# Four small attentions of a perceiver network: exponentials by head on ScalarE, groups of four heads, division on the output, and one barrier fewer per stage

## The reference

```python
def layer_norm(x):
    ...
    return (x - mu) / jnp.sqrt(var + EPS)
def pattention(x, K, V):                 # K, V: 256 rows, for f 1024 rows
    a = softmax(EMB ** -0.5 * einsum('btc,nc->btn', x, K)); return einsum('btn,nc->btc', a, V)
def causal_sdpa(q, k, v):
    scores = einsum('bhqd,bhkd->bhqk', q, k) / sqrt(d)
    scores = where(tril, scores, -inf); attn = softmax(scores); return einsum('bhqk,bhkd->bhqd', attn, v)
h = layer_norm(x_in)                     # k, q, v = pattention(h, kK, kV), (h, qK, qV), (h, vK, vV)
...                                      # o = causal_sdpa(q, k, v); x2 = x_in + pattention(o, pK, pV)
...                                      # y = x2 + pattention(layer_norm(x2), fK, fV)
```

```python
scores = jnp.einsum('bhqd,bkd->bhqk', q, k) / sqrt(128)
scores = jnp.where(causal, scores, finfo.min)
attn = jnp.einsum('bhqk,bkd->bhqd', softmax(scores), v)
return attn.transpose(...).reshape(...) @ Wo
```

## Time and profile before

| | us |
|---|---|
| three runs | 1778.31, 1773.97, 1777.92 |
| median | 1777.92 |
| profiled execution | 1778.89, span 1777.1, mean TensorE clock 0.881 |
| PE / DVE / ACT / POOL busy | 1433.1 (81%) / 1001.7 (56%) / 700.0 (39%) / 96.5 (5%) |

### The profile page before, as it was taken

One profiled execution on the slowest core, in us unless ns is written; L12 is line 12 of the kernel. 1 busy time (PEld: TensorE's weight loads), 2 busy tenths in 40 slices (PEclk: granted clock), 3 DMA queues, 4 the chain that ended last, 5 costly groups with the idle time before them and its releaser, 6 DMA issues. The chain is left out here.

```text
span 1777.1 us, 28179 instructions
## 1 busy us (share of the span) xinstructions
PE 1433.1 (81%) x10760; PEld 1067.2 (60%) x10760; DVE 1001.7 (56%) x2900; ACT 700.0 (39%) x1524; POOL 96.5 (5%) x90
## 2 busy tenths in 40 slices
PE   7999999776598447799999999999983654647975
PEld 6979889554376233367776777777762532445763
DVE  5645444584565312277777777777756945343333
ACT  5735445212121110167667667666761010112211
POOL 2300000000000210200000000001000000000000
PEclk9999999888799659799999999999996565658997
DMA  9944333100331749410000000000002007007810
GB/s 320 327 164 160 118 111 140 53 1 20 139 131 56 249 153 350 180 59 33 33 33 33 33 33 33 33 32 33 2 1 116 1 0 301 0 0 261 277 57 4
DMA packets 61783, 181.15 MB, mean 102 GB/s; under 512 B 7249, under 2 KB 41169, under 8 KB 60369
## 3 DMA queue, kind: packets, MB, share of 16 engines
q1 hardware_dynamic: 56864, 156.77, 24.7%
q0 software_dynamic: 4352, 16.78, 2.6%
q10 hardware_dynamic: 432, 5.80, 0.8%
HBM read 178.68 MB, written 0.66 MB: 101 GB/s over the span
## 5 line engine op out<-in xcount | busy, mean ns | idle before, releaser
L1733 ACT ACTIVATE cross_s<-cross_s,cross_shift 128x896 f32<-128x896 f32 x224 | 215.1, 1031 | 35.2 <-DVE cross_shift L1813 35.2
L1727 ACT COPY cross_eT<-cross_ring 128x512 f32<-128x512 f32 x280 | 153.2, 591 | 144.9 <-PE cross_ring L1653 144.9
L1653 PE MATMUL cross_ring<-consts,cross_s 128*128 128x128 f32 x1568 | 199.4, 280 | 8.7 <-ACT cross_s L1733 8.7
L1653 PEld LDWEIGHTS cross_ring<-consts,cross_s 128*128 128x128 f32 x1568 | 170.7, 142 | 59.1 <-issue 43.8
L1804 DVE CUSTOM_DVE_ANT_0 cross_s<-cross_scores,cross_mask,cross_top 128x448 f32<-128x448 f32 x224 | 141.3, 680 | 84.3 <-PE cross_scores L1645 84.3
L374 ACT ACTIVATE slots_probs<-slots_scores,slots_bias,ctx_rinv 128x128 f32<-128x128 f32 x294 | 130.2, 460 | 109.0 <-DVE slots_bias L418 109.0
L1804 DVE CUSTOM_DVE_ANT_0 cross_s<-cross_scores,cross_mask,cross_half_max 128x448 f32<-128x448 f32 x224 | 141.3, 681 | 18.8 <-PE cross_scores L1645 18.8
L134 PE MATMUL slots_scores<-slots_qkT,slots_ctxT 128*128 128x128 f32 x1176 | 139.8, 277 | 9.1 <-DMA slots_ctxT<-in_ctxT 8.2
L134 PEld LDWEIGHTS slots_scores<-slots_qkT,slots_ctxT 128*128 128x128 f32 x1176 | 138.3, 194 | 13.0 <-DMA slots_ctxT<-in_ctxT 9.2
L324 PE MATMUL slots_attended<-ctx_rows,slots_probs 128*128 128x257 f32 x588 | 135.2, 380 | 1.4 <-DVE slots_pooled L432 1.4
L1645 PE MATMUL cross_scores<-cross_keysT,cross_qz 32*128 32x448 f32 x896 | 119.0, 589 | 0.8 <-DVE cross_keysT L1778 0.8
(11 more groups left out here) (742 smaller groups left out, 2114.3 us busy)
## 6 DMA issues: line engine op xcount, KB each, us to landing
slots_ctxT<-in_ctxT SPq DMA_DIRECT2D x42, 896.0 KB, 4.6
ctx_rows<-in_ctx_rows SPq DMA_DIRECT2D x28, 896.0 KB, 7.6
padded_ctxT<-in_ctxT SPq DMA_DIRECT2D x14, 896.0 KB, 4.6
cross_ctxT<-in_ctxT SPq DMA_DIRECT2D x14, 896.0 KB, 4.6
plain_ctxT<-in_ctxT SPq DMA_DIRECT2D x14, 896.0 KB, 4.7
ring_w<-in_moe_w POOLq DMA_DIRECT2D x12, 1024.0 KB, 17.8
ring_w<-in_moe_w SPq DMA_DIRECT2D x12, 1024.0 KB, 11.8
local_layers<-in_w_local SPq DMA_DIRECT2D x2, 4806.0 KB, 15.3
```

The lines of the kernel that those rows point to most:

```text
L1653: last = pe.transpose(bank(("turn", u, t))[:, j * P:(j + 1) * P], s_buf[:, u % 2, j, t * P:(t + 1) * P], K.ident)
L1727: act.copy(eT[:, u % 2, t], bank(item)).then_inc(st("emptied_act"), 1)
L1733: act.activation(rows, rows, ACT.Exp, bias=shift[:, u % 2, j:j + 1], scale=SCALE).then_inc(st("exp"), 1)
```

## The change

1. The second barrier at a stage's end is gone. GpSimd alone clears the semaphores after the block's barrier, and a new stage takes none of the numbers that the stage before it used (`semaphore()`, `Stage.cleared`).
2. `root_table` issues one square root, whose result nobody reads, at the end of ScalarE's stream in eleven stages; after it the set with Sqrt is the one loaded. The program has 45 table loads before and after.
3. In the four attentions the maximum (negated) is taken per group of four heads (`maxima_vector`), ScalarE reads the scores from PSUM and writes each head's exponential with that head's maximum as bias (`exponentials_scalar`: 16 in patt and in folded; 8 per layer in local and 8 in mqa, these with the sum in `accum_out`), TensorE turns a group as soon as its four are there (`turn_group`), VectorE copies it (`copies_vector`), and TensorE multiplies the group before it (`attend16`). Scores are scaled in a copy that was there anyway (hT, qT, oT, kT). The causal mask is added by TensorE: a product of identity and mask into the bank with `stop=False`, then the scores with `start=False`. The division moves to o: in patt and folded v has a 17th column of ones, whose product is the sum (`outputs16`); in local o is multiplied by the reciprocal of the sums. In mqa the probabilities are still divided, per group.
4. Patt: the two layer norms are one (one ScalarE call takes both square roots), the k, q, v, p and f softmaxes use bias and `accum_out`, f by halves; the quantising is cut into six pieces, 42 steps, dealt out by `Q_SPLIT`. The counts of idle products change: 4 at the start (5 before), none in front of the transposes of k, q, v and probabilities, later 2, 4, 3 for 3, 3, 9 and 1.
5. Folded: GpSimd fetches three slots of the ring; the fourth is fetched by SP at the start of moe. v is copied by ScalarE. Idle products are added: 4 at the start, 14 before the transposes of q and k, 3 after, 18 while o is away.
6. Local: masks and 16 idle products before the rotated q and k are turned, 3 after the scores; the copy of qkT in two parts. Mqa: masks and 2 idle products at the start, 4 after the scores, the last products by halves.

The core of the diff (patt's, folded's and local's streams to the part that is used below):

```diff
@@ Stage
     def __exit__(self, kind, *_):
         if kind is None:
-            self.nc.clear_and_free_semaphores(list(self.sems.values()))
-            self.nc.all_engine_barrier()
+            mine = list(self.sems.values())
+            Stage.cleared = [s.num for s in mine]
+            self.nc.clear_and_free_semaphores(mine)
         self.mem.close()
...
+def root_table(act, K):
+
+    act.activation(K.unused, K.ident[:, 0:1], ACT.Sqrt)
...
+def exponentials_scalar(act, st, tag, e, src, top, of, groups):
+
+    per = of // groups
+    for g in range(groups):
+        act.wait_ge(st(f"{tag}_top"), g + 1)
+        for h in range(g * per, (g + 1) * per):
+            last = act.activation(e[:, h], src[:, h], ACT.Exp, bias=top[:, h:h + 1])
+        last.then_inc(st(f"{tag}_exp"), 1)
+
+
+def maxima_vector(dve, st, tag, src, top, groups):
+
+    per = top.shape[1] // groups
+    for g in range(groups):
+        some = slice(g * per, (g + 1) * per)
+        dve.wait_ge(st(f"{tag}_scores"), g + 1)
+        dve.tensor_reduce(top[:, some], src[:, some], X_AXIS, ALU.max, negate=True).then_inc(st(f"{tag}_top"), 1)
...
+def attend16(pe, K, st, tag, heads, headsT, pr, prT, v, o_mm):
+
+    def attend(g):
+        pe.wait_ge(st(f"{tag}_probsT"), g + 1)
+        for hd in range(4 * g, 4 * g + 4):
+            last = pe.matmul(o_mm[:, hd], prT[:, hd], v[:, hd], start=True, stop=True)
+        return last
+
+    for g in range(4):
+        turn_group(pe, K, st, tag, headsT, pr, g, 4)
+        if g:
+            attend(g - 1)
+    attend(3).then_inc(st("o_mm"), 1)
+
+
+def outputs16(dve, link, st, o, o_mm, inverse):
+
+    dve.wait_ge(st("o_mm"), 1)
+    link(dve.reciprocal(inverse, o_mm[:, :, HEAD16]))
+    dve.tensor_tensor(o[:, :].rearrange("p (h d) -> p h d", d=HEAD16), o_mm[:, :, 0:HEAD16], spread(inverse, HEAD16), ALU.mult).then_inc(st("o"), 1)
...
-Q_PIECES = 3
+Q_PIECES = 6
 Q_BLOCKS = QCOLS // QBLOCK // Q_PIECES
 Q_STEPS = 7
+Q_SPLIT = (4, 8, 4, 2, 2, 4, 4, 4, 10)
@@ patt, TensorE
+                def mask(g):
+                    pe.matmul(heads[:, 4 * g:4 * g + 4], K.ident, repeat(K.causal, 4), start=True, stop=False)
...
+                pe.wait_ge(st("v"), 2)
+                attend16(pe, K, st, "sdpa", heads, headsT, pr, prT, v, o_mm)
@@ patt, VectorE
+                maxima_vector(dve, st, "sdpa", heads, small[:, 0, :], 4)
+                quantise_some(Q_SPLIT[0])
+                copies_vector(dve, st, "sdpa", prT, headsT, 4)
+                quantise_some(Q_SPLIT[1])
+                outputs16(dve, link, st, o, o_mm, small[:, 1, :])
+                quantise_some(Q_SPLIT[2])
@@ folded, ScalarE and GpSimd
-                softmax_scalar(act, st, "sdpa", pr[:, :], HEAD16 ** -0.5)
-                act.wait_ge(st("sdpa_probsT_mm"), 1)
-                act.copy(prT[:, 8:16], headsT[:, 8:16]).then_inc(st("sdpa_probsT"), 1)
+                act.wait_ge(st("folded_in"), 16)
+                act.copy(v[:, :, 0:HEAD16], folded[:, :, 2]).then_inc(st("v"), 1)
+                exponentials_scalar(act, st, "sdpa", pr, heads, small[:, 0, :], HEADS16, 4)
+                root_table(act, K)
...
                 pool.wait_ge(st("folded_in"), 16)
-                for p in range(SLOTS):
-                    if p == SLOTS - 1:
-                        pool.wait_ge(st("o2_in"), 16)
+                for p in range(SLOTS - 1):
                     K.ring.fetch_w1(pool, p)
                     K.ring.fetch_w2(pool, p)
@@ moe, SP
+                K.ring.fetch_w1(sp, SLOTS - 1)
+                K.ring.fetch_w2(sp, SLOTS - 1)
                 for p in range(SLOTS, COUPLES):
@@ local, TensorE
+                    pe.wait_ge(st("copied"), n + 1)
+                    for bank in range(2):
+                        pe.matmul(three(big[0][:, bank * 512:(bank + 1) * 512]), K.ident, repeat(K.causal, 4), start=True, stop=False)
+                    idle_products(pe, K, big[2], 16)
                     pe.wait_ge(st("rotated"), n + 1)
...
+                    turn_group(pe, K, st, f"sdpa{n}", three(big[1][:, :]), pr, 0, IC)
+                    turn_group(pe, K, st, f"sdpa{n}", three(big[1][:, :]), pr, 1, IC)
+                    attend(0)
+                    attend(1).then_inc(st("o_mm"), 1)
@@ mqa, TensorE
+                for j in range(2):
+                    pe.matmul(s_mm[:, 4 * j:4 * j + 4], K.ident, repeat(K.causal, 4), start=True, stop=False)
+                idle_products(pe, K, mm2, 2)
                 pe.wait_ge(st("ln_done"), 1)
```

403 lines of the change are left out of this document (239 added, 164 removed).

## The result

The changed kernel takes 1701.20 us (median of four runs, 1691.99 to 1704.30), the kernel before 1775.95 (1773.39 to 1778.31): ratio 0.957, 95% interval 0.953 to 0.961. That is 75 us less where 63 were forecast.

What follows compares the result with a forecast made beforehand. Prediction: the small-attention stages are bound by a chain handing one tile from engine to engine. Savings of 7.3 + 0.8 + 16.9 + 11.5 + 18.4 + 8.3 = 63.2 us give 1715 us; whole range 1701 to 1733.

Steps and rivals of the forecast that it cites:

- the barrier: Stage exits: dropping the second of two barriers, some 0.6 us each, saves 7.3 us (4 to 8.4).
- the table: Layer norms opening delta and hashed: loading the square-root table ahead saves 0.4 us each, 0.8 in all (0 to 1).
- patt: Patt stage: 3.6 up to the last score, 12.6 from there to o, 0.7 after; 16.9 us saved (14 to 19).
- the smaller slack: End of patt: quantising no longer hides in softmax waits; its last ten steps, 7.5 us, stand ahead of the final residual.
- the mechanism of folded: Folded: 16 us shorter attention gains nothing because o's store waits on the ring; removing GpSimd's drain gives most of 11.5 us.
- Rival B: Folded: o's store gets through in bunches and lands by 36 us, saving another 7; 1708 us, chance 15 of 100.
- The pause of 11.84: Between folded's x_kept and moe's start: the wait on GpSimd's drain shrinks to one barrier, 0.55 us, saving 11.3.
- the time at which the store lands: Folded: o's store, interleaved with the expert ring, takes about 19 us and lands near 54.5 us after the start.
- moe unchanged: Expert stage: fetching the fourth slot at its start counted as nothing; without cover it would cost up to 11 us.
- local: Two local layers: shorter softmax chain and faster TensorE clock save 9.2 us per layer, 18.4 in all.
- the clock: Local: idle products keep TensorE nearer full clock through transposes, scores and wo's product, saving 1.8 us per layer.
- Mqa: Mqa stage: opening costs 2.8, products gain 4.7, softmax 5.0, scaling 1.4; 8.3 us saved (6.9 to 9.1).

Runs made afterwards that it cites:

- the second execution: The unmodified changed kernel measured and profiled again in a later set: 1696.48 us, ratio 0.957 to the kernel before.
- the experiment with the ring behind the store: Changed kernel, but in folded GpSimd fetches only expert slot 0; SP issues slots 1 and 2 behind the read of o: 1691.57 us, ratio 0.9527.
- the reverse experiment: Changed kernel with its unused column in a 16-column buffer, so the expert ring begins 32 bytes past a multiple of 64: 1703.09 us, ratio 0.9598.
- the two executions with a slow local: Changed kernel with the second barrier put back (1706.89 us), and with expert slot 1 issued behind o's read and slot 2 at moe's start (1688.15 us).

## Why the prediction was right or wrong

- **Right, the barrier and the table.** VectorE's waits shrink by 7.0 us for the first (7.3 forecast); the times give 5.7 to 10.4. The second is visible as 0.4 us a time and lost in the noise.
- **Right, patt.** Last score after 21.1 us (20.2 forecast), o 13.9 behind it (13.65), so after 35.0 (33.85); exponentials at 0.26 (0.28). The stage is 15.9 shorter (16.9 forecast), in the second execution 20.1, at a higher clock. That the smaller slack puts the quantising at the end came out.
- **Right, the mechanism of folded.** The attention's 18 us fell on nothing: the store was issued 18 us earlier and took 20.6. Rival B is out, since the store's packets go one for one with the ring's; the experiment with the ring behind the store shows it from the other side, 3.0 us. What the Trainium skill says of whole packets of some 9 to 17 descriptors from one queue at a time ("DMA: Bandwidth & Descriptors", "Queues, rings and completion order") this trace does not bear out: a first turn of nine on each of 16 engines would be 144 of the store's packets at once, and 39 run in its first 0.6 us. The prediction had also drawn too much from the page: if both queues' packets hold as many descriptors, the counts are equal by its rule too, and that is not B. The pause of 11.84 became 0.52.
- **Wrong, the time at which the store lands and with it the ring's end.** "It still lands when the ring does, near 54.5 after the start": it landed at 50.0. 2.8 of the 4.5 are the ring's rate, which the prediction took as given. It rose from 369 to 409 GB/s, since a buffer of one column, listed in the diff and costed at nothing, moved the ring onto a multiple of 256 bytes: moved off it again, the store lands at 52.9. The other 1.6 are a mistake of the count: 54.5 is the landing of the kernel before, whose store was issued so late that it ended behind the ring, and the ring itself was through at 52.6. (The prediction's own numbers give 31.9 + 19 = 50.9 for the interleaving, and the store had been issued 4.9 us ahead of the ring's end and not 3.5.)
- **Wrong, moe unchanged.** The same place in SBUF is worth 3.0 us in folded and 5.5 in moe by the reverse experiment (59.3 and 76.2), 6 to 7 in the times. Moe's waits for the ring were in the trace. What the prediction did say of moe holds: off the multiple it takes 76.2 with the fourth slot fetched at its start and 75.4 before, so that slot costs 1 us at most.
- **Wrong in size, local.** Forecast 14.8 for the chains of two layers and 3.6 for the clock. The chain from mask to o is 6.3 us (1460.25 to 1466.57), forecast 7.3, before 14.7. The term "scores and wo's product behind it run nearer to full clock: 1.8" was mis-sized: in the first layer turning, scores, o's turning and wo's product alone lost 0.9 + 0.9 + 0.5 + 1.8 = 4.1, and the q, k, v product of the second layer 1.7 (7.11 to 5.42). By the experiments the idle products are worth 6.8 and the attention without them 21.5. The step that failed: I counted what idle products do between the rotation and wo and gave the attention its chain alone; the shorter waits of the attention raise the clock too (0.64 before, 0.78 with either edit, 0.90 with both). Wo's product shows both at work: 3.5 with either edit alone, 1.99 with both. Idle products and short waits are not sufficient, as the two executions with a slow local show.
- **Mqa** 10.9 for 8.3. The products that the forecast had faster gained 2.3 and not 4.7 (scores 3.17 to 2.64, those with v 3.74 to 1.98, wo's 3.73 in both), while those it did not name gained about as much (q 4.63 to 3.74, the turning of the probabilities 1.97 to 1.27, k's and v's products 2.26 to 1.29). The opening costs 1.9 and not 2.8 (the first product of the chain starts 4.0 us after the start, before 2.2), and 0.5 is the barrier's. The remaining 1.2 no experiment assigns.
- Not settled: why the clock fell within local in two executions of ten, what sets it in patt, and why slots varies by 5 us between executions.

## What to carry to other kernels

Treat a new buffer in a diff as a change to every transfer into what is allocated behind it: compute the address modulo 256 bytes. A transfer in small pieces issued beside a long one on another queue costs what is left of the long one; issue the long one behind it, up to where the next stage waits for the bytes. A queue's rate in the trace of before is no constant: ask what sets it. And count TensorE's clock over the whole stage: both filling a wait and shortening waits raise it, each was worth more here than had been counted for it, and their gains added. Look at more than one execution, since the clock can fall in the same code.
